# A two-stage attention block on one core: GpSimd issues a third of the stack transfers, and the rotation of groups 4 to 7 is built from a second product

## The reference

```
x = rmsnorm(tokens) * (1 + 0.1 tanh(scale)) + shift      # scale, shift from the condition
q, k, v = split(x @ qkv_w.T + qkv_b)                     # 16 heads of 8 features
q, k = rope(q), rope(k)     # pairs (even, odd) -> (even cos - odd sin, even sin + odd cos)
tokens = tokens + attention(q, k, v) @ out_w.T + out_b
cq = rmsnorm(tokens) @ wq.T + bq;  ck, cv = rmsnorm(side) @ wk.T + bk, @ wv.T + bv
update = attention(cq, ck, cv) @ mha_out_w.T + mha_out_b  # masked by valid rows
tokens = tokens + sigmoid([tokens, update] @ gate_w.T + gate_b) * update
out = tokens + (silu(g) * val) @ down_w.T + down_b,  g, val = split(rmsnorm(tokens) @ gu_w.T + gu_b)
```

## Time and profile before

| | |
|---|---|
| median of 3 runs | 519.72 us (514.06, 519.72, 522.11) |
| the profiled execution | 517.94 us, span 516.1 us |
| granted TensorE clock, mean | 0.937 of full |
| TensorE busy | 442.1 us (86%) |
| TensorE weight loads | 308.3 us (60%) |
| VectorE busy | 350.1 us (68%) |
| ScalarE busy | 290.4 us (56%) |
| GpSimd busy | 190.8 us (37%) |
| SP's DMA queue (q1) | 60050 packets, 49.07 MB, 32.2% of 16 engines |

### The profile page before, as it was taken

One profiled execution on the slowest core, in us unless ns is written; L12 is line 12 of the kernel. 1 busy time (PEld: TensorE's weight loads), 2 busy tenths in 40 slices (PEclk: granted clock), 3 DMA queues, 4 the chain that ended last, 5 costly groups with the idle time before them and its releaser, 6 DMA issues.

```text
span 516.1 us, 13226 instructions
## 1 busy us (share of the span) xinstructions
PE 442.1 (86%) x5219; PEld 308.3 (60%) x5219; DVE 350.1 (68%) x655; ACT 290.4 (56%) x644; POOL 190.8 (37%) x184
## 2 busy tenths in 40 slices
PE   3546889878897986999989988999999969999897
PEld 2115375756675664666577655866586748565664
DVE  2326655878885896698677866767748856856565
ACT  4321364577566664777576648486636744556243
POOL 4451140614433163528381828254542542000010
PEclk9975778899997999799999999999989999999999
DMA  3355442354353445344443443425140320000001
GB/s 77 87 174 174 131 122 88 100 162 151 100 162 107 140 121 153 103 128 121 131 137 108 117 140 97 153 67 163 43 149 25 98 92 3 23 3 22 22 1 42
DMA packets 62942, 52.04 MB, mean 101 GB/s; under 512 B 3803, under 2 KB 61728, under 8 KB 62880
## 3 DMA queue, kind: packets, MB, share of 16 engines
q1 hardware_dynamic: 60050, 49.07, 32.2%
q10 hardware_dynamic: 2830, 2.12, 1.4%
HBM read 8.55 MB, written 2.11 MB: 21 GB/s over the span
## 4 chain that ended last, share of the span: by engine, by line
PE 52%; DVE 11%; DMA 10%; ACT 8%; issue 8%; SPq 5%; POOL 4%; ACTq 1%; DVEq 0%; POOLq 0%
PE ps_o L403 8%; PE ps_a L366 7%; PE ps_g L320 7%; PE ps_b L386 6%; PE ps_g L461 5%; SPq L658 4%; DMA k_st<-part_k 4%; DVE top L1087 4%; PE ps_g L444 4%; PE ps_g L353 3%; DMA q_st<-top_t 3%; ACT probs L902 2%; DMA s_in<-in_fside_BxSxS 1%; ACT turned_in L838 1%; PE ps_g L418 1%
## 5 line engine op out<-in xcount | busy, mean ns | idle before, releaser
L1087 DVE TENSOR_REDUCE top<-ps_a 128x4 f32<-128x512 f32 x256 | 169.6, 680 | 106.1 <-PE ps_a L366 104.8
L902 ACT ACTIVATE probs<-ps_b 128x512 f32<-128x512 f32 x256 | 151.3, 595 | 143.6 <-PE ps_b L386 139.5
L366 PE MATMUL ps_a<-k_st,q_st 73*128 73x128 bf16 x1024 | 105.0, 228 | 27.8 <-DMA k_st<-part_k 15.0
L366 PEld LDWEIGHTS ps_a<-k_st,q_st 73*128 73x128 bf16 x1024 | 69.8, 101 | 79.5 <-issue 59.9
L386 PE MATMUL ps_b<-q_st,k_st 75*128 75x128 bf16 x1024 | 102.0, 223 | 9.4 <-ACT probs L902 7.5
L386 PEld LDWEIGHTS ps_b<-q_st,k_st 75*128 75x128 bf16 x1024 | 69.6, 99 | 18.5 <-issue 9.2
L403 PE MATMUL ps_o<-probs,v_pad 128*32 128x128 f32 x2048 | 73.3, 287 | 0.0
L403 PEld LDWEIGHTS ps_o<-probs,v_pad 128*32 128x32 f32 x2048 | 55.3, 115 | 24.1 <-issue 14.7
L728 POOL TENSOR_TENSOR f<-f 128x4 f32<-128x4 f32 x16 | 16.6, 1038 | 98.8 <-DVE f L1136 98.8
L320 PE MATMUL ps_g<-norm,w_t 128*128 128x512 f32 x66 | 37.1, 647 | 1.2 <-DVE hid L1178 1.2
L320 PE MATMUL ps_g<-turned_in,w_t 128*128 128x512 f32 x48 | 30.3, 717 | 5.0 <-ACT turned_in L838 4.8
(11 more groups left out here) (197 smaller groups left out, 677.6 us busy)
## 6 DMA issues: line engine op xcount, KB each, us to landing
q_st<-part_q SPq DMA_DIRECT2D x126, 128.0 KB
k_st<-part_k SPq DMA_DIRECT2D x120, 128.0 KB
x_in<-in_x SPq DMA_DIRECT2D x16, 256.0 KB, 4.5
q_st<-hid SPq DMA_DIRECT2D x18, 128.0 KB
s_in<-in_fside_BxSxS SPq DMA_DIRECT2D x8, 256.0 KB, 5.7
out<-t SPq DMA_DIRECT2D x8, 256.0 KB, 2.3
k_st<-hid SPq DMA_DIRECT2D x12, 128.0 KB
swap_q<-part_q SPq DMA_DIRECT2D x8, 128.0 KB, 2.3
```

The source lines that it names most:

```text
L366: mm = pe.matmul(ps_a[q % 2][:, j * S:(j + 1) * S], st[0][i][0:R_MAX, h, b * S:(b + 1) * S], st[1][i][0:R_MAX, h, b * S:(b + 1) * S], star ...
L902: act.activation(probs[:, n % 2, q * T:(q + 1) * T], ps_b[q % 2][:, :], ACT.Exp, scale=SCALE).then_inc(exp_done, 1)
L1087: dve.tensor_reduce(top[:, n // 2 % 2, n % 2, QH * q:QH * (q + 1)], ps_a[q % 2][:, :].rearrange("p (h k) -> p h k", h=QH), AX.X, ALU.max). ...
```

## The change

1. The lowest parts' transfers (o = 2) leave SP, and for groups 0 and 1 ScalarE too. GpSimd issues them (`stack_lo`): after it has made the lowest part, it waits for its own result and issues three transfers. In a self phase the six of q and k stand together behind the lowest part of k; in a cross phase they stand three and three. They count on semaphores of their own, `lo_stacked`, and `stacks_in` waits for both.
2. Groups 4 to 7 do as groups 0 to 3: a second product on TensorE for q and for k, sine and cosine parts by VectorE in one step, a subtraction by GpSimd at steps s_prep + 7 and + 9 instead of + 9 and + 11. The exchange transfers, their semaphores and the space for them go; the sine part lies in `sin_q` and `upd`. VectorE waits for `gate_mul` before the k's sine part, where SP did.
3. For groups 4 to 7 the splitting and its transfers stand one step earlier on ScalarE, GpSimd and SP.

The core of the diff, in the order buffers, waits, TensorE, SP, GpSimd (four pieces), ScalarE (`stack_k`), VectorE (two pieces):

```diff
-        swap_to = [sb("swap_q", [D, T]), upd]
+        sin_q = sb("sin_q", [D, T])
...
         def sined(r, p):
-            if p < 4:
-                return (unit_th, norm3)[r]
-            return part[r][:, 0:2, :].rearrange("d p t -> d (p t)").bitcast(F32)
+            return (unit_th, norm3)[r] if p < 4 else (sin_q, upd)[r]
...
-            eng.wait_ge(stacked[r][p % 2], 16 * PRODUCTS * (p // 2 + 1))
+            eng.wait_ge(stacked[r][p % 2], 16 * (PRODUCTS - PARTS) * (p // 2 + 1))
+            eng.wait_ge(lo_stacked[r][p % 2], 16 * PARTS * (p // 2 + 1))
...
-                        if g < 4:
-                            swapped_product(("qs", g), t, 3, W_Q, g)
+                        swapped_product(("qs", g), t, 3, W_Q, g)
...
-                    if g >= 4 and t == s_prep(g) + 7:
-                        swap(0, g)
-                    if g >= 4 and t == s_prep(g) + 9:
-                        swap(1, g)
                     for o in range(PARTS):
-                        if t == s_prep(g) + (11, 14, 15)[o]:
+                        if o < 2 and t == s_prep(g) + (11, 14)[o] - (g >= 4):
                             stack(0, o, sp_at)
-                        if t == s_prep(g) + (13, 15, 16)[o]:
+                        if o < 2 and t == s_prep(g) + (13, 15)[o] - (g >= 4):
                             if g > 1 or o == 0:
                                 stack(1, o, sp_at)
-                        if t == ck_prep(g) + (8, 10, 11)[o]:
+                        if o < 2 and t == ck_prep(g) + (8, 10)[o]:
                             stack(1, o, cp_at)
-                        if t == cq_prep(g) + (11, 14, 15)[o]:
+                        if o < 2 and t == cq_prep(g) + (11, 14)[o]:
                             stack(0, o, cp_at)
...
+            def stack_lo(r, p):
+                wait(pool, b_done, NQ * NG * (p - 2))
+                pool.wait_ge(lo_set[r], p + 1)
+                for other in range(PARTS):
+                    product = PARTS * 2 + other if r == 0 else PARTS * other + 2
+                    pool.dma_start(st[r][p % SETS][product:R_MASK:PRODUCTS, :, :], parts(r, p)[:, 2, :]
+                                   ).then_inc(lo_stacked[r][p % 2], 16)
...
-                    if t == s_prep(g) + 15:
+                    if t == s_prep(g) + 15 - (g >= 4):
                         take_mid(1, sp_at)
+                        stack_lo(0, sp_at)
+                        stack_lo(1, sp_at)
...
                     if t == ck_prep(g) + 10:
                         take_mid(1, cp_at)
+                        stack_lo(1, cp_at)
...
                     if t == cq_prep(g) + 14:
                         take_mid(0, cp_at)
+                        stack_lo(0, cp_at)
...
-                for o in (1, 2):
-                    for p in range(2):
-                        if t == s_prep(p) + (0, 14, 16)[o]:
-                            stack_k(o, p)
+                for p in range(2):
+                    if t == s_prep(p) + 14:
+                        stack_k(1, p)
...
+                    if r == 1 and g >= 4:
+                        wait(dve, gate_mul, sum(post(e, "residual") < s_prep(g) + 8 for e in range(G)))
...
-                            if t == s_prep(g) + 6 + 2 * r + (which if g >= 4 else 0):
+                            if t == s_prep(g) + 6 + 2 * r:
                                 rope(r, g, which)
```

52 lines of the change are left out of this document (17 added, 35 removed).

## The result

The changed kernel took 538.7 us (median of four runs, 535.8 to 545.0), the kernel before 517.1 us in runs on the same chip: a ratio of 1.040, 95% interval 1.033 to 1.048. It is slower, by about 21 us; the forecast was 509.0 us and its range ended at 524. Some executions of each kernel run longer at a lower granted clock; the ratios in this document leave them out, the medians and ranges do not. In the profiled executions 541.25 us stand against 517.94 us.

What follows compares the result with a forecast made beforehand. TensorE's matrix work was taken to bound late phases, with waits for stack transfers and half clock behind them elsewhere. Gains of 20.6 less costs of 11.7 took 8.9 us from the profiled 517.9 us: 509.0 us, range 501 to 524.

Steps and rivals of the forecast that it cites:

- the part on GpSimd's issues: GpSimd issuing the lowest parts costs 0 us at the start and norm roots, and gains 5.6 us before phase 15.
- D: Time one transfer issue holds GpSimd, taken as 1.1 us; SP's takes 0.65 us.
- Cheap issues: Rival: an issue takes GpSimd about 0.65 us, as SP, so the start gains 5 us: 504 us; chance 0.17.
- GpSimd's queue becomes the bound: Rival: each issue holds GpSimd 2 us or more, so start and norm roots come late: 534 us; chance 0.13.
- Same eight engines: Rival: lowest parts run on engines SP's fill, so waits before phases 15, 3 and 9 stay: 515.6 us; chance 0.15.
- (a): Start: twelve issues stand before the root of group 2's norm, at 48.3 with D = 1.1: 0 us; -5 at 0.65.
- (b): Cross attention's norm root behind six issues, room for 7.4 us in phase 7: 0 us at 1.1 each.
- (c): Last cross attention: q's lowest stack part lands at 417.4, before TensorE's arrival at 419.4; gain 5.6 us.
- The stalls before phases 5 and 7: Group 4 self attention and group 5: stacks land in time, gain 5.7 + 6.8 = 12.5 us, half clock included.
- The eight products: Added q and k products of groups 4 to 7 on TensorE: 8.1 us cost, 4 us if all in VectorE's shadow.
- The bank wait of the second gate product: Groups 6 and 7, steps 113 and 145: TensorE waits for a PSUM bank read by `hidden`, 1.2 us each.
- The prediction's share of 0.88: DMA engines' share at 250 GB/s when a load runs beside a stack, against 0.58 at 180 GB/s during a stack.

Runs made afterwards that it cites:

- GpSimd's half: Kernel before with only the 84 lowest parts' transfers issued by GpSimd, SyncE still moving the exchanged halves of groups 4 to 7: 533.84 us, ratio 1.031.
- an eighth of the data: GpSimd's half with all 84 issues in place, each moving an eighth of its data from phase 3 on: 513.63 us, ratio 0.993 to the kernel before.
- ScalarE's issues: Kernel before with ScalarE instead of SyncE issuing q's lowest parts' transfers in phases 3, 5, 7 and 15: 515.91 us, ratio 1.000.
- The hold of 1.07 us an issue: The products' half with GpSimd held by six operations per stack where it had issued, no transfer added: 547.36 us, ratio 1.059 to the kernel before.
- the products' half: Changed kernel with SyncE and ScalarE issuing the lowest parts again, GpSimd none; second product and earlier steps kept: 524.0 us, ratio 1.011 to the kernel before.
- the first pair of kernels: GpSimd issues in phases 6, 8, 10 to 14 only, k's cross-phase ones behind or ahead of the top rows' transfer: 521.86 us behind, 524.61 us ahead.
- the second: The first pair of kernels with ScalarE issuing q's lowest parts in phases 3, 5, 7 and 15: 518.41 us behind, 526.69 us ahead.

## Why the prediction was wrong

**The step that failed** is the part on GpSimd's issues. By its own terms GpSimd's half gains 6.6 us (5.6 before phase 15, 1.0 before phases 3 and 9, nothing lost at D = 1.1); measured alone, it cost 16 us (ratio 1.031). D was 0.60 us, better than the forecast's 1.1 and just below the cheap end of its bounds, so the price of an issue is not what failed. Three things are. First, the part gave no price to what GpSimd's transfers do to other transfers: the top rows' transfer that ScalarE issues at the same time took 7.8 us in place of 3.7, and TensorE waits for it in mid-phase (7.5 against 1.9 us in all). Second, it took 2.3 us for the landing, the figure of SyncE's exchange in another shape; no row showed the term for a stack transfer, and GpSimd's took 5.0 to 5.5 us. Third, it looked for what stands behind the issues on GpSimd's queue only at the start and at the root of the cross attention's norm, and missed the MLP's unit and the root behind k's issues in phase 12: 4 to 5 us, which stayed with an eighth of the data and came without any transfer.

With an eighth of the data 20 us of GpSimd's half went (533.8 to 513.6), some of them waits that the kernel before has as well, so the data is the larger part of the cost. How the 16 us divide exactly stays open: the place of k's issues is worth 8.3 us, about half of it each way, and nearly half of it is half clock behind the waits. In the trace of GpSimd's half, phase 0 begins 0.7 us earlier than in the kernel before; the phases 1 to 5 are 9.6 us longer together, phase 7 is 2.6 us longer, phase 12 4.7 and phase 13 1.2. So the start did not lose the time. What lengthens the phases 1 to 5 was not taken apart; leaving to SyncE the six phases whose stacks have no slack gave back nothing measurable. That the packets of 4096 bytes are what delays the small transfer was not tested by itself either.

**The rivals.** All of them priced the issue or the engines' share. "Cheap issues" had the right D and the wrong end, 504 us. "GpSimd's queue becomes the bound" (534 us) came nearest to the 538.7 measured, but mostly by luck: it needed issues of 2 us, and they take 0.60; a held queue is worth a part of the loss, at another place than it said. "Same eight engines" foresaw that the wait before phase 15 stays (2.83 of 3.86 us did), and that a stack's landing is not set by SyncE's queue, with which ScalarE's issues agree (3.86 to 2.72 us); which engines the transfers used, no trace shows.

**(a) The start.** At D = 0.65 the forecast had 5 us gained; phase 0 began at 39.16 us in place of 40.75, 1.6 us gained. The root of group 2's norm started at 46.86, nearly where D = 1.1 had put it (48.3), because VectorE was late for it, not GpSimd's queue.

**(b) What stands behind GpSimd's issues.** The forecast gave the root of the cross attention's norm room for 7.4 us, so that six issues at 1.1 us cost nothing. The hold of 1.07 us an issue cost 23 us, with 10.2 us of TensorE waiting for that root. The slack was overstated. A likely reason, only argued, is that it was counted from the time at which the exchange would be gone, 4.5 us earlier, while the sum of group 5 in the changed kernel came at 187.65 against 184.44 before. It hurt little, since D was 0.60: the wait for the root was 0.5 us in the changed kernel.

**(c) Phase 15.** Forecast 5.6 us gained; 1.0 us of idle time was, and the clock behind it stayed at 0.50 for 3.4 us.

**The stalls before phases 5 and 7.** In the products' half both went, so the 4.5 us that the exchange took were rightly read. Of the 12.5 us only the idle part (2.70 + 4.39 = 7.1 us) went: over the whole span the time lost to the clock stayed (34.9 against 34.5 us) instead of falling by the 5.4 us forecast. Of this term the size was wrong, and the sum of the half, by its own terms 2.3 us faster (12.5 + 1.5 less 8.1, 1.2 and 2.4), was 6 us slower. This is the second, smaller miss. The two halves' misses, 22.6 and 8.3 us, are 30.9 us together; the measured median is 29.7 above the forecast.

**The eight products.** Forecast 8.1, measured about 5 by themselves: between the two bounds. **The bank wait of the second gate product**: the mechanism and both places were right, the size 1.79 us in place of 1.2. VectorE's reduction takes 0.68 us as before.

The Trainium skill was weighed in the prediction ("DMA: Bandwidth & Descriptors", sections "Rules for kernel authors" and "Why a DMA increments its semaphore by 16 and not by 1"). That spreading issues over engines brings no bandwidth agrees with ScalarE's issues, ratio 1.000. That GpSimd's transfers would use idle engines beside SyncE's eight was the half that I leaned on; whichever engines they used, they cost more engine time per byte (75 against 54 us for each MB) and stood in the others' way, and no trace here separates the engines. The prediction's share of 0.88 "when a load runs beside" a stack was misread: between 54 and 58 us SyncE's queue has loads only, its last stack transfer having been issued at 43.6 us; the load beside a stack is in the window of 0.58. With hardly anything but stack transfers under way, from 406 to 416 us in the kernel before, the share is 0.51 at 160 GB/s, as much as eight engines' worth.

## What to carry to other kernels

Moving a transfer to another queue is not free because its issue is cheap. Look up who else's transfer is in flight at that moment, and whether TensorE waits for it, above all for the small ones with no slack. Then go through everything that stands behind the issue on its new queue, in every phase and not only in the one that looks tight (here 8.3 us for three steps, about half for each reason). Keeping every issue and cutting the data tests the first; but compare phase by phase, since the cut also shortens waits that were there before and so hides a price that stays. And do not book the half clock behind a wait as gain when the wait goes; in this kernel the time lost to the clock stayed as it was.

## What the runs showed of the hardware

- A transfer of 128 KB between on-chip tiles that GpSimd issues went out in 32 packets of 4096 bytes, whose records last 0.291 us on average, with 48 small ones; SyncE's goes in packets of 1024 bytes, 0.053 us each. On the two queues as a whole that is 75 against 54 us of engine time for each MB. It landed 5.0 to 5.5 us after its issue at the median (3.1 to 10.2).
- Issuing it held GpSimd for 0.60 us, no longer than SyncE (0.61 at the median), with VectorE busy 66% of the span.
- GpSimd's queue held without any transfer cost some 3 us for 67 us of holding and 23 us for 103 us; where an issue stood before operations that the next phase's work waited for, 28.7 us of one phase became 33.
- A transfer of 16 KB by ScalarE took 3.7 us when it was issued ahead of three such transfers, and 7.8 us when among them (one instance each).
- Half clock is not proportional to the wait before it: behind a wait of 3.86 us one phase lost 1.7 us (28.5 us long), behind 3.53 us in another kernel the same phase took 33.1 us. No run here shows what decides between the two. One such episode is the likely reason why the first pair of kernels differed by 2.7 us and the second by 8.3.
